# Rows scaled by chunks at the end of a delta stage, and the next stage's first tokens prepared inside it

## The reference, cut to what matters

```python
x = x + attention(layernorm(x))
x = x + recurrent(layernorm(x))
x = x + delta(layernorm(x))
x = x + recurrent(layernorm(x))

def step(c, xt):                     # recurrent, over the 4 sequences
    ft = sigmoid(xt @ wf.T + c @ uf.T + bf)
    it = sigmoid(xt @ wi.T + c @ ui.T + bi)
    gt = tanh(xt @ wc.T + c @ uc.T + bc)
    return ft * c + it * gt
h = tanh(x @ wo.T + c_final @ uo.T + bo)

def chunk(S, qc, kc, vc, bc):        # delta, per head and sequence
    kb = kc * bc[:, None]
    A = tril(kb @ kc.T, -1)
    U = solve_triangular(eye + A, vc * bc[:, None] - kb @ S, lower=True)
    o = qc @ S + tril(qc @ kc.T) @ U
    return S + kc.T @ U, o
rms = o * rsqrt(mean(o * o, axis=-1) + 1e-5)
out = (rms * norm_w * silu(g)) @ Wo
```

## Time and profile before

| | us |
|---|---|
| median of three runs | 1347.2 |
| the profiled execution | 1354.21 |
| its span, first to last instruction | 1352.1 |
| TensorE busy | 1193.1 (88%) |
| VectorE busy | 853.9 (63%) |
| ScalarE busy | 628.1 (46%) |
| GpSimd busy | 400.7 (30%) |

### The profile page before, as it was taken

The page is one execution under the profiler, slowest core; times in us unless marked ns, Lnnn a source line. Parts: engine busy times, 40 slices in busy tenths (PEclk is TensorE's granted clock), DMA queues, the critical chain, the costliest instruction groups (busy, mean ns, idle before and its releaser), DMA issues. The chain is left out here.

```text
span 1352.1 us, 32378 instructions
## 1 busy us (share of the span) xinstructions
PE 1193.1 (88%) x13506; PEld 744.2 (55%) x13506; DVE 853.9 (63%) x1879; ACT 628.1 (46%) x1289; POOL 400.7 (30%) x632
## 2 busy tenths in 40 slices
PE   6769999999999999998999957768898787599995
PEld 3334444444444444444888844436676666388884
DVE  5756767676787887844553466787786632265346
ACT  4336666676666666667322334323343222152223
POOL 5411414142200000003531135555445331343210
PEclk9889999999999999998999977888999899799998
DMA  6882425354544444100000000111111110000003
GB/s 204 158 196 35 88 38 91 50 83 60 83 49 49 61 55 60 19 2 1 1 0 1 24 8 9 28 31 34 35 35 37 31 31 8 1 1 0 0 1 124
DMA packets 78753, 61.65 MB, mean 46 GB/s; under 512 B 41360, under 2 KB 65552, under 8 KB 78480
## 3 DMA queue, kind: packets, MB, share of 16 engines
q1 hardware_dynamic: 77456, 57.18, 23.7%
q10 hardware_dynamic: 1152, 2.41, 0.6%
HBM read 38.20 MB, written 20.97 MB: 44 GB/s over the span
## 5 line engine op out<-in xcount | busy, mean ns | idle before, releaser
L728 ACT ACTIVATE weights<-psum 128x512 f32<-128x512 f32 (+1 forms) x608 | 322.7, 584 | 160.3 <-PE psum L629 158.3
L778 DVE TENSOR_REDUCE maxima<-psum 128x1 f32<-128x512 f32 (+3 forms) x432 | 262.5, 664 | 52.4 <-PE psum L551 51.4
L629 PE MATMUL psum<-q_stack,k_stack 99*128 99x512 bf16 (+3 forms) x768 | 223.3, 327 | 1.3 <-ACT weights L728 1.1
L551 PE MATMUL psum<-k_stack,q_stack 96*128 96x512 bf16 (+3 forms) x768 | 212.7, 328 | 2.3 <-DVE maxima L778 2.0
L646 PE MATMUL psum<-weights,v_rows 128*17 128x512 f32 (+3 forms) x1536 | 161.2, 491 | 0.1
L523 POOL TENSOR_TENSOR residual<-residual,att_o 128x256 f32<-128x256 f32 x32 | 23.2, 725 | 355.9 <-DVE att_o L811 355.9
L966 PE MATMUL psum<-f_xT,f_weights_hi 128*128 128x512 f32 x384 | 122.4, 400 | 2.0 <-DVE f_hidden L1100 2.0
L778 DVE TENSOR_REDUCE negmax<-psum 128x1 f32<-128x384 f32 (+3 forms) x176 | 102.4, 636 | 28.7 <-PE psum L551 27.0
L1067 DVE TENSOR_TENSOR f_state<-f_gates 128x512 f32<-128x512 f32 x32 | 28.2, 881 | 142.1 <-POOL f_gates L929 86.5
L629 PEld LDWEIGHTS psum<-q_stack,k_stack 99*128 99x128 bf16 x768 | 72.3, 98 | 82.7 <-ACT weights L728 38.0
L1016 ACT ACTIVATE f_gates<-psum,ffn_biases 128x512 f32<-128x512 f32 x72 | 49.4, 689 | 141.0 <-PE psum L972 131.9
(11 more groups left out here) (164 smaller groups left out, 2210.9 us busy)
## 6 DMA issues: line engine op xcount, KB each, us to landing
qk_parts<-a_parts SPq DMA_DIRECT2D x32, 384.0 KB, 4.0
q_stack<-qk_parts SPq DMA_DIRECT2D x90, 128.0 KB, 7.3
k_stack<-qk_parts SPq DMA_DIRECT2D x90, 128.0 KB, 8.0
residual<-in_x SPq DMA_DIRECT2D x8, 512.0 KB, 7.4
out_x<-residual SPq DMA_DIRECT2D x8, 512.0 KB, 2.9
ffn_weights<-in_ffn_w ACTq DMA_DIRECT2D x1, 2048.0 KB, 9.0
systems<-d_a_rows SPq DMA_DIRECT2D x32, 64.0 KB, 1.8
d_systems<-systems SPq DMA_DIRECT2D x4, 512.0 KB, 3.5
```

Source lines behind the costliest of these rows:

```text
L551: m = e.matmul(out[:, i * width:(i + 1) * width], self.qst[st][0:self.ROWS, h, qb * P:(qb + 1) * P], self.kst[st][0:self.ROWS, h, k0:k0 + ...
L629: m = e.matmul(out[:, j * width:(j + 1) * width], self.kst[st][0:self.ROWS + self.MAX_ROWS, h, kb * P:(kb + 1) * P], self.qst[st][0:self.R ...
L728: e.activation(self.weights[n % 2][:, heads[0]:heads[-1] + 1, 0:width], bank[self.score_bank[n, i]][:, 0:len(heads) * width].rearrange("p ...
L778: e.tensor_reduce(to, bank[self.bank[item]][:, 0:len(heads) * width].rearrange("p (h x) -> p h x", h=len(heads)), AXIS_X, ALU.max, negate= ...
```

## The change

At the end of the delta stage:

- GpSimd's scaling becomes a function `normalise(Go, part)`. Groups 0 to 6 are still scaled whole, now in slot 4Go+22; the last group is scaled chunk by chunk, in slots 46 to 49, each chunk after its own sum.
- The guests on VectorE and GpSimd move from slot 51 to slot 46 (LAST_SLOT - 10), and they are groups 0 and 2 of the second recurrent stage now, where it was group 0 alone. VectorE normalises group 1 at slot 52, three tiles, and the fourth behind the first addition of the last group.
- TensorE turns group 0 at the head of slot 49, into banks 2 and 3. ScalarE and VectorE split its tokens at slot 50 and weight matrices 0 and 1 at slot 52.

In both recurrent stages:

- TensorE turns group 1 between the second and the third gate of group 0, no longer ahead of them.
- ScalarE and VectorE split in the order tokens 0, matrices 0 to 3, tokens 1, matrices 4 to 7.

```diff
+    def turn_bank(self, p, kt):
+        return self.k.bank[kt + 2 if p == 0 and self.early else kt]
+    def first_tensor(self, e, unmet):
+        for kt in range(KT):
+            self.ln.tensor(e, unmet, 0, kt, self.turn_bank(0, kt), None)
+    def split_scalar(self, e, unmet, n):
+        k = self.k
+        free = self.before if not self.early else self.early["first_weights" if n < 2 else "weights"]
...
@@ Ffn.tensor
-        turn(0)
-        turn(1)
+        if not self.early:
+            for w in unmet(*self.before):
+                e.wait_ge(*w)
+            self.first_tensor(e, unmet)
         for p, (t, j) in enumerate(self.ORDER):
             x = self.xT[p % 3]
             for n, (gate, mt) in enumerate(self.gate_order(p)):
+                if p == 0 and n == 2:
+                    for w in unmet(*self.before):
+                        e.wait_ge(*w)
+                    turn(1)
@@ Ffn.vector (Ffn.scalar has the same order)
-        turn(0)
-        split_weights(0)
-        turn(1)
-        for n in range(1, 8):
-            split_weights(n)
-        self.ln.vector(e, unmet, 2)
+        if not self.early:
+            self.turn_vector(e, unmet, 0)
+            for n in range(2):
+                self.split_vector(e, unmet, n)
+        for n in range(2, 8):
+            if n == 4:
+                self.turn_vector(e, unmet, 1)
+            self.split_vector(e, unmet, n)
+        if 2 not in self.ahead:
+            self.ln.vector(e, unmet, 2)
@@ Delta.gpsimd
-            if slot == LAST_SLOT - 5:
+            if slot == LAST_SLOT - 10:
                 self.guests["gpsimd"](e, unmet, [norm["turned"](QB - 1, KT - 1)])
...
-            Go, ostep = self.output(slot)
-            if Go is not None and ostep == 0:
...
+            Go, left = divmod(slot - LAG_S - TPG, TPG)
+            if left == 0 and 0 <= Go < QB - 1:
+                self.normalise(e, unmet, Go, range(TPG))
+            c = slot - LAG_S
+            if self.chunk(c) and c // TPG == QB - 1:
+                self.normalise(e, unmet, QB - 1, range(c % TPG, c % TPG + 1))
@@ Delta.tensor
+            if slot == LAST_SLOT - 7:
+                self.guests["first_tensor"](e, unmet)
@@ Delta.scalar
+            if slot == LAST_SLOT - 6:
+                self.guests["turn_scalar"](e, unmet, 0)
+            if slot == LAST_SLOT - 4:
+                for n in range(2):
+                    self.guests["split_scalar"](e, unmet, n)
@@ Delta.vector
-            if slot == LAST_SLOT - 5:
+            if slot == LAST_SLOT - 10:
                 self.guests["vector"](e, unmet)
+            if slot == LAST_SLOT - 6:
+                self.guests["turn_vector"](e, unmet, 0)
+            if slot == LAST_SLOT - 4:
+                self.guests["next_vector"](e, unmet, slice(0, TPG - 1))
+                for n in range(2):
+                    self.guests["split_vector"](e, unmet, n)
...
+                    if Go == QB - 1 and b == 0:
+                        self.guests["next_vector"](e, unmet, slice(TPG - 1, TPG))
@@ build
-        first = Ffn(k, "f1_", attention.updated, attention.ends(), 2)
+        first = Ffn(k, "f1_", attention.updated, attention.ends(), (0, 1))
-        second = Ffn(k, "f2_", delta.updated, delta.ends(), 1)
+        second = Ffn(k, "f2_", delta.updated, delta.ends(), (0, 2), delta.front_end())
```

More of the change, by code:

```diff
@@ L841, with __init__ @@
     BESIDE = {(GROUPS - 2, 1): 0, (GROUPS - 2, 2): 1, (GROUPS - 1, 0): 2, (GROUPS - 1, 1): 3}
-    def __init__(self, k, tag, x_ready, before, ahead):
-        self.k, self.before, self.ahead, self.guests = k, before, ahead, {}
+    def __init__(self, k, tag, x_ready, before, ahead, early=None):
+        self.k, self.before, self.ahead, self.guests, self.early = k, before, ahead, {}, early
         with ExitStack() as ctx:
@@ L906, in ahead_vector @@
     def ahead_vector(self, e, unmet):
-        for p in range(self.ahead):
+        for p in self.ahead:
             self.ln.vector(e, unmet, p)
@@ L914, in ahead_gpsimd, with next_vector, turn_scalar, turn_vector @@
             e.wait_ge(*w)
-        for p in range(self.ahead):
+        for p in self.ahead:
             self.ln.gpsimd(e, unmet, p)
+    def next_vector(self, e, unmet, part):
+        self.ln.vector(e, unmet, 1, part)
+    def turn_bank(self, p, kt):
[3 more added lines that the diff above has]
+            self.ln.tensor(e, unmet, 0, kt, self.turn_bank(0, kt), None)
+    def turn_scalar(self, e, unmet, p):
+        s = self.s
+        for kt in range(KT):
+            for w in unmet(self.ln.s["turned"](p, kt), *(self.early["tokens"] if p == 0 and self.early else self.before),
+                           s["hidden_mm"](p - 3, 1) if p >= 3 else None):
+                e.wait_ge(*w)
+            e.activation(self.xT[p % 3][:, 0, kt, :], self.turn_bank(p, kt)[:, :], ACT.Copy).then_inc(*s["xT_hi"].did(p, kt))
+    def turn_vector(self, e, unmet, p):
+        s, x = self.s, self.xT[p % 3]
+        for kt in range(KT):
+            for w in unmet(s["xT_hi"](p, kt)):
+                e.wait_ge(*w)
+            e.tensor_tensor(x[:, 1, kt, :], self.turn_bank(p, kt)[:, :], x[:, 0, kt, :], ALU.subtract).then_inc(*s["xT_lo"].did(p, kt))
+    def split_scalar(self, e, unmet, n):
+        k = self.k
+        free = self.before if not self.early else self.early["first_weights" if n < 2 else "weights"]
+        for w in unmet(k.s["ffn_w_in"](), *free):
+            e.wait_ge(*w)
+        e.activation(self.w_parts[0][:, n, :, :], k.ffn_w[:, n, :, :], ACT.Copy).then_inc(*self.s["w_hi"].did(n))
+    def split_vector(self, e, unmet, n):
+        for w in unmet(self.s["w_hi"](n)):
+            e.wait_ge(*w)
+        e.tensor_tensor(self.w_parts[1][:, n, :, :], self.k.ffn_w[:, n, :, :], self.w_parts[0][:, n, :, :], ALU.subtract
+                        ).then_inc(*self.s["w_lo"].did(n))
     def gpsimd(self, e, unmet):
         k, s = self.k, self.s
-        for p in range(self.ahead, 3):
-            self.ln.gpsimd(e, unmet, p)
+        for p in range(3):
+            if p not in self.ahead:
+                self.ln.gpsimd(e, unmet, p)
         for p in range(GROUPS):
@@ L1238, in ends, with front_end @@
         return [self.s["out_mm"](G, B - 1), self.s["oT"](G, TPG - 1), self.s["joined"](G, B - 1), self.s["o_norm"](G, TPG - 1)]
+    def front_end(self):
+        c, G = CHUNKS - 1, QB - 1
+        front = [self.s["vg_mm"](c), self.s["conv"](G, KT - 1, self.TAPS - 1)]
+        return {"tokens": front, "first_weights": front + [self.s["au_mm"](c)],
+                "weights": [self.s["au_mm"](c), self.s["o_norm"](G, TPG - 1)]}
     @staticmethod
@@ L1736, in build @@
         delta.guests |= {"vector_end": first.vector_end, "scalar_end": first.scalar_output}
+        delta.guests |= {"first_tensor": second.first_tensor, "turn_scalar": second.turn_scalar, "turn_vector": second.turn_vector,
+                         "split_scalar": second.split_scalar, "split_vector": second.split_vector,
+                         "next_vector": second.next_vector}
         def sync(e, unmet):
```

84 lines of the change are left out of this document (34 added, 50 removed).

## The result

| | before | after |
|---|---|---|
| median of 5 runs, us | 1347.2 (1343.69 to 1352.83) | 1337.05 (1332.56 to 1339.84) |
| ratio to before, 95% interval | | 0.9898 (0.9873 to 0.9924) |
| profiled execution, us | 1354.21 | 1332.56 |
| its span, us | 1352.1 | 1330.5 |

The change makes the kernel 1.0% faster. By the medians it is 10.2 us or 0.8% (a quotient of 0.9925, just outside the interval of the recorded ratio), so the size is known to some 3 us and no better. On two other chips the ratio was 0.9921 (0.9908 to 0.9934) and 0.9901 (0.9878 to 0.9923). The two profiled executions differ by 21.6 us, twice what the medians do (the one before is the longest time of its kernel on this chip, the one after the shortest of its own), so the changed kernel was profiled three times and the kernel before twice, and each place is compared over all of them.

What follows compares the result with a forecast made beforehand. The prediction took the kernel to be bound by TensorE, with a chain over GpSimd and VectorE holding it at delta's end. -19.0 + 3.5 + 0.9 = -14.6 us from 1347.2 gave 1332.6 us, range 1328.5 to 1340.

Steps and rivals of the forecast that it cites:

- the clock rival: Tail after delta: TensorE's clock falls there, so the end gains only 13.7 us; 1337.9 us in all, chance 0.19.
- End of delta: From the last chunk to the second stage's fifth gate of the next group: 19.0 us gained, between 13.7 and 19.7.
- Its signs: End of delta: last scaling within 3 us of last sum, TensorE idle below 1, products 3.7 us, first gate at once.
- First recurrent stage: Turning group 1 later delays VectorE's last split, and the shift arrives undiminished: 3.5 us lost, between 1.6 and 4.3.
- One sign of being wrong: End of delta: the prediction is wrong if TensorE waits for VectorE's additions at the last group; no size given.
- My sign for this stage: First recurrent stage: the wait for VectorE's copy of the output part grows from 1.40 us to about 3.
- Inside delta: Group 0's earlier scaling delays the key factors at slot 24: 0.9 us lost, between 0 and 2.3.
- the later scalings: Delta slots 26 and 30: scaling groups 1 and 2 meets GpSimd idle times of 4.25 and 6.11 us, costing nothing.
- Sum: Whole kernel: -19.0 + 3.5 + 0.9 = -14.6 us, giving 1332.6 us from the median 1347.2.
- The first stage hides its shift: First recurrent stage: slack in VectorE's chain makes the 3.5 us loss 0; 1329.1 us in all, chance 0.12.
- Held by GpSimd: Last group: a chunk's scaling costs a group's 6.4 us, rows ready 9.8 us late; 1342.4 us, chance 0.03.
- The slower one: Slots 22, 26 and 30: early scalings hold the key factors 6.4 us each, 19.2 together; 1350.9 us, chance 0.03.

Runs made afterwards that it cites:

- guests_only: The kernel before, with only the guests' layer norm on VectorE and GpSimd moved five slots of delta earlier; 0.9920 of the kernel before.
- no_chunks: The kernel after, but the last group scaled whole after its last sum instead of chunk by chunk; 0.9911 of the kernel before.
- first_only: The kernel before, with only the new order of turning and splitting in the first recurrent stage; 1.0044 of the kernel before.
- late_scaling: The kernel after, with groups 0 to 5 scaled two slots later, as before the change; 0.9888 of the kernel before.
- ln_early: The kernel after, with VectorE's statistics of group 2 taken ahead of its turning of group 1 in the first stage; 0.9842 of the kernel before.
- old_ln: The kernel after with the first stage's old order, and group 2's statistics ahead of VectorE's first turning there; 0.9833 of the kernel before.
- first_old: The kernel after, with the first recurrent stage in its old order, both groups turned before any split; 0.9865 of the kernel before.
- before_again: The kernel before, unchanged, run once more for one profile on another chip; 1353.06 us.

## Why the prediction was right

Right, in the time (1332.6 against 1337.05, in the range) and in its mechanisms. Two sizes were off, in opposite directions, and partly cancel. The time alone would not tell the forecast from the clock rival (1337.9); the profiles do, with the clock at 1.00 in the last group's products and the first gates.

- **End of delta, 19.0 gained (13.7 to 19.7).** Measured over the profiles: T from 62.4 to 41.5 in the mean, and 0.95 for the turning ahead of it: 20.0. Its signs came as named: last scaling ready 2.4 us after the last chunk's sum (1151.42 to 1153.83; within 3), TensorE's idle time under 1 us, products at 3.76, the first gate directly behind them. From the first to the fifth gate of the next group it was 19.4 us (1162.29 to 1181.72), for 18 to 19: the 0.77 us wait for group 1's layer norm was not in the sum. GpSimd made that norm's four products beside VectorE's splits (last section). One sign of being wrong came by its letter: TensorE waits for an addition of VectorE at the last group, for 0.39 us at 1157.02, inside the turning. It is small, and guests_only has it too. But where the gain sits I had not separated: the guests' place made 11 to 13 of it, turning inside delta 7 to 9, the chunks nothing.
- **First recurrent stage, 3.5 lost (1.6 to 4.3).** This is the term that was mis-sized: F grew by 5.8 (38.2 against 32.4). The part that I worked out, up to the fifth gate, is there: 24.41 us before, 27.74, 29.07 and 29.09 after, so +3.3 to +4.7. VectorE's last split ended 10.1 us after the first transposes before, and 13.1, 14.4 and 14.5 after. In two of the three profiles of the kernel after the clock came back later than before, counted from the first transposes (in the third, with these at 626.81, it was 0.50 until 636; in the kernel before, at 627.63, until 634), and these two are the ones that lost 4.7. This agrees with what the Trainium skill says ("TensorE: Matmul & The Clock Gate", Part 1), that activity releases the slow clock. The first profile came back as early as before. What I left out stands behind the fifth gate: the two waits, 1.5 us and 2.1, are followed by a new fall of the clock, and from the fifth gate to the next turning it takes 7.24 to 7.32 us for 5.73: 1.5 more. All six profiles that have both waits have this fall (after three times, no_chunks, first_only, late_scaling), and none of the seven others: in ln_early and old_ln, without the waits, and in first_old, with one of 1.76 us, the clock stayed at 1.00. Whether it takes both waits or the longer one alone, no run separates. My sign for this stage was off as well: the wait for the copy of the output part grew from 1.40 to 2.11 us and not to 3, since the new wait at group 2's turning took 1.48 of it first.
- **Inside delta, 0.9 lost (0 to 2.3).** VectorE's wait for the factors at slot 24 grew from 2.85 to 5.35 us (5 predicted; 5.13 and 5.14 in the two other profiles):

```profile
982.33 0.42 DVE L1690 TENSOR_TENSOR d_attnT_k_kb_v<-d_k_raw,d_k_factors 128x256 f32<-128x256 f32 x1 [5.35 <-POOL d_k_factors L1417]
```

  Slot 25 grew by 0.8. I had called the later scalings free; in the means over all profiles slot 46 grew by 1.1, slot 47 lost 0.6 of it again, and slot 32 gained 0.3. Together 1.0, of which only the step at slot 25 stands clear of the scatter.
- **Sum.** -20.0 + 5.8 + 1.0 = -13.2 us, for -14.6 predicted. The three ratios, taken on 1354.2, are -13.8, -10.7 and -13.4: -12.6 in the mean. The medians differ by 10.2, 11.1 and 13.6: 11.6 in the mean. On the chip of the result the gain was thus 10 to 14 us, and the forecast somewhat too high.
- **Rivals.** The clock did fall in the new tail, in one of three profiles and for 1.3 us, not 6. "The first stage hides its shift" fell with first_old and first_only. "Held by GpSimd" fell twice over: even a whole scaling does not hold the last group. (Its start of 1143.5 is not what its terms add up to, 1127.0 + 7.8 + 6.4 = 1141.2; it was 1144.10, since the norms began only at 1129.83. Nothing else rests on it.) The slower one priced 6.4 us in three places; 0.8 and 1.1 came in two.

Open is what moves the slots in the middle of delta by up to 2 us between executions. From the first chunk to the last the stage took 224.2 and 220.2 us before, and 218.2, 223.3 and 224.3 after, turning included; the 6 us that the first pair of profiles shows there is not the change's.

## What to carry to other kernels

Where an engine waits for a helper, first look whether the helper stands idle earlier and a guest blocks it: here two moved constants made 11 to 13 of the 20 us at the end of delta. When an order is changed for one engine, list everything queued behind the moved piece on the engine that pays (here VectorE's statistics, and through them GpSimd's queue); the same statistics moved into the new gap gave the loss back and more. Before a helper's step is cut, look at what runs beside it: here its first part lay beside other products, its last part already came in pieces, each of which freed a part of the next step, and cutting it brought nothing.

## What the runs showed of the hardware

- After waits of 1.5 and 2.1 us TensorE's clock went from 2.4 to 1.2 GHz in all three profiles of the kernel after (0.50 in 658 to 660 in two of them, 0.57 there in the other) and in the three other kernels that have both waits, and not behind one wait of 1.26 to 1.76 us (before, before_again, guests_only, first_old). The price was 1.5 us, as much as a wait itself.
- GpSimd's power cost 1.04 us for 4 columns and 2.93 for 16, so cutting a scaling of four chunks by chunk makes it dearer in all, 4 x 2.4 us in place of 6.4.
- GpSimd's four products of a layer norm took 3.11 us beside VectorE's splits of matrices 2 and 3 (1.49 us for two, 1.26 elsewhere), and 2.18 without them, as in guests_only. The first two of the four took the extra time (1.07 and 0.97 us, the others 0.55). Of the kernel after:

```profile
1162.90 3.11 POOL L241 TENSOR_SCALAR normed<-residual,ln_negmean,ln_rstd 128x256 f32<-128x256 f32 x4
```

```profile
1163.01 1.49 DVE L956 TENSOR_TENSOR f_weights_lo<-ffn_weights,f_weights_hi 128x512 fp32r<-128x512 f32 x2
```
